# First attention of a float32 block: bf16 thirds on 96 array rows replaced by two rounded f32 halves on 52 rows, with scores and maxima on different halves of the array

## What is computed

```python
qkv = q @ in_proj_weight.T + in_proj_bias          # 4096 x 768
qh, kh, vh = heads of 16 columns, 16 heads
qh = qh / math.sqrt(d)                              # d = 16
scores = jnp.einsum('bhid,bhjd->bhij', qh, kh)      # 4096 x 4096 a head
rel = jnp.clip(pos[None, :] - pos[:, None], -K, K) + K          # K = 64
bias = take_along_axis(einsum('bhid,rd->bhir', qh, rel_pe), rel)
attn = jax.nn.softmax(scores + bias, axis=-1)
out = jnp.einsum('bhij,bhjd->bhid', attn, vh)
```

## Time and profile before

| | us |
|---|---|
| median of 3 runs | 5778.08 (5756.49 to 5778.12) |
| profiled execution, its own time | 5783.44 |
| its span (first to last instruction) | 5781.8 |
| TensorE matmul busy | 5294.7 |
| VectorE busy | 4105.4 |
| ScalarE busy | 3109.6 |
| GpSimd busy | 953.5 |

### The profile page before, as it was taken

How to read it: one execution, slowest core, us unless ns; L and a number is a source line. 1 busy time by engine, 2 the same in 40 slices (tenths; PEclk the granted TensorE clock), 3 DMA queues, 4 the chain that set the end, 5 groups by cost and what they waited for, 6 DMA issues and landing times. The chain is left out here.

```text
span 5781.8 us, 113252 instructions
## 1 busy us (share of the span) xinstructions
PE 5294.7 (92%) x33984; PEld 2681.2 (46%) x33984; DVE 4105.4 (71%) x8598; ACT 3109.6 (54%) x4537; POOL 953.5 (16%) x704
## 2 busy tenths in 40 slices
PE   7499999999999999999999999985999898999895
PEld 3233333333333333333333333332888654888653
DVE  4388888888888888888888888832777433777434
ACT  3256666666666666666666666630555312565310
POOL 0111111111111111111111111101333101333100
PEclk8589999999999999999999999975999899999997
DMA  6511112111111111112111111112000000000000
GB/s 166 141 40 53 48 54 56 48 53 54 50 53 53 48 54 55 48 53 54 50 53 53 47 52 47 52 43 91 1 0 0 16 0 16 1 0 0 30 0 29
DMA packets 203462, 254.49 MB, mean 44 GB/s; under 512 B 71086, under 2 KB 132852, under 8 KB 201588
## 3 DMA queue, kind: packets, MB, share of 16 engines
q1 hardware_dynamic: 199524, 232.98, 14.3%
q0 software_dynamic: 3856, 20.45, 1.3%
HBM read 210.73 MB, written 42.47 MB: 44 GB/s over the span
## 5 line engine op out<-in xcount | busy, mean ns | idle before, releaser
L745 DVE TENSOR_REDUCE group_max<-shared_ps 128x1 f32<-128x512 f32 x4096 | 2684.7, 688 | 586.7 <-PE shared_ps L469 484.2
L622 ACT ACTIVATE probs<-scores 128x1024 f32<-128x1024 f32 x2048 | 2012.3, 1021 | 1052.9 <-PE scores L495 673.7
L469 PE MATMUL shared_ps<-keys,max_queries 96*128 96x512 bf16 x4096 | 1436.1, 385 | 3.2 <-issue 1.7
L495 PE MATMUL scores<-queries,keys 98*128 98x512 bf16 (+3 forms) x4096 | 1218.5, 372 | 86.6 <-ACT probs L622 85.6
L510 PE MATMUL out_ps<-probs,values 128*17 128x512 f32 x8192 | 1089.2, 604 | 0.4 <-ACT probs L622 0.4
L469 PEld LDWEIGHTS shared_ps<-keys,max_queries 96*128 96x128 bf16 x4096 | 396.1, 97 | 1123.5 <-DVE group_max L745 507.9
L215 POOL TENSOR_TENSOR near_window<-near_bias,one_f 128x1536 bf16<-128x1536 f32 x128 | 351.5, 2746 | 2953.7 <-DVE max_parts L739 2305.8
L495 PEld LDWEIGHTS scores<-queries,keys 98*128 98x128 bf16 x4096 | 360.3, 98 | 465.7 <-ACT probs L622 236.9
L1303 PE MATMUL quad<-h_T,w 128*128 128x512 f32 (+1 forms) x768 | 344.3, 599 | 1.9 <-ACT h_T L1417 1.9
L521 PE MATMUL shared_ps<-block_q,block_table 96*128 96x32 bf16 x4096 | 271.5, 233 | 65.2 <-POOL block_q L406 65.2
L521 PEld LDWEIGHTS shared_ps<-block_q,block_table 96*128 96x128 bf16 x4096 | 231.3, 114 | 171.8 <-issue 122.4
(11 more groups left out here) (186 smaller groups left out, 5639.0 us busy)
## 6 DMA issues: line engine op xcount, KB each, us to landing
keys<-k_parts SPq DMA_DIRECT2D x384, 96.0 KB, 2.1
values<-v_wide SPq DMA_DIRECT2D x128, 272.0 KB, 2.7
keys<-k_parts SPq DMA_DIRECT2D x384, 64.0 KB, 2.0
keys<-k_parts SPq DMA_DIRECT2D x128, 132.0 KB, 2.4
q_stack<-part SPq DMA_DIRECT2D x96, 128.0 KB
k_parts<-part SPq DMA_DIRECT2D x96, 128.0 KB
queries<-q_stack SPq DMA_DIRECT2D x128, 96.0 KB, 2.2
max_queries<-q_stack SPq DMA_DIRECT2D x128, 96.0 KB, 2.3
```

The lines of the kernel that those rows point to most:

```text
L469: mm = pe.matmul(bank, max_queries[par][:, t * P:(t + 1) * P], keys[par][0:ROWS, (t + TPC * g) * P:(t + TPC * (g + 1)) * P], start=True, s ...
L495: mm = pe.matmul(out[:, 0:cut], keys[par][:, c * P:(c + 1) * P], queries[par][:, 0:cut], start=True, stop=True)
L622: act.activation(probs[s % 4][:], scores[s % 2][:], ACT.Exp).then_inc(exp_done, 1)
L745: dve.tensor_reduce(group_max[par][:, k:k + 1], bank, AX.X, ALU.max).then_inc(max_read, 1)
```

## The change

q and k are each cut into two values that the f32r format (f32 rounded for a single pass through the array) holds exactly, `high` and `low`. A product is high x high + low x high + high x low, which takes 3 x 16 rows; two rows carry the edge term of the bias (`edge_rows`, from a new small matmul in the projection), two the maximum: 52 rows. The same operands are kept twice, on partitions 0 to 51 and on 64 to 115. Scores use the lower copy, maxima the upper (`max_pair`). The two kinds alternate in the program.

The keys of a head (all 4096) stay on chip for its eight steps; loads are by head. `max_ps` has two slots of two banks, and VectorE reduces both banks with one instruction (`pair_max`, 128x1024), 16 a step in place of 32 of 128x512. `score_ps` is a ring of three single banks that carries scores, the prepared bias and the maximum rows; the exponential is 32 instructions of 128x512 a step in place of 16 of 128x1024. The near columns of the scores are spread over the order of the tiles (`ORDER`). GpSimd copies the maximum row to the second side (`copy_max`). The projection is unrolled and its staging buffers are double; v is stored once. The loop body of `attend` has 16 steps in place of 2. The later stages are the same code.

```diff
@@ -37,13 +37,12 @@
 TPC = CH // P
-Q_PARTS = (0, 0, 0, 1, 1, 2)
 K_RUNS = (3, 2, 1)
 MROWS = 2
+KROWS = 2 * MROWS + 3 * D
 VW = D + 1
 SLAB = 2 * P
...
+    NEAR = (0, 1, 2, 3, 4, TILES - 1)
+    ORDER = [5, 0, 1, 6, 2, 3, 7, 4] + list(range(8, TILES))
+    NEAR_SPAN = {0: (0, 192, 1, 64), 1: (64, 320, 2, 0), 2: (192, 448, 3, 0), 3: (320, 512, 4, 0),
+                 4: (448, 512, 5, 0), TILES - 1: (0, 64, 0, 192)}
+    BIAS_TURN = {0: 0, 1: 1}
+    ROWS_TURN = 4
+    STEP = []
+    for turn in range(QUADS):
+        if turn == ROWS_TURN:
+            STEP.append(("rows", 0))
+        STEP += [("score", (4 * (turn + 2) + i) % TILES) for i in range(4)]
+        if turn in BIAS_TURN:
+            STEP.append(("bias", BIAS_TURN[turn]))
+    STEP.append(None)
+    RING = 3
+    S_START = 2 * NEXT_GEN + 1 + 8
...
-        scores = [ps(f"scores{i}", [P, 2, CH]) for i in range(2)]
+        score_ps = [ps(f"score_ps{i}", [P, CH]) for i in range(RING)]
+        max_ps = [ps(f"max_ps{i}", [P, 2, CH]) for i in range(2)]
...
-        shared_ps = [ps(f"shared_ps{i}", [P, CH]) for i in range(3)]
...
+            def load_keys(h, par):
+                part = k_parts[bass.ds(h, 1)].rearrange("a r n -> (a r) n")
+                for base in (P // 2, 0):
+                    sp.dma_start(keys[par][base + 4:base + 4 + D, :].bitcast(F32), part[0:D]).then_inc(keys_in[par], 16)
+                    sp.dma_start(keys[par][base + 4 + D:base + KROWS, :].bitcast(F32), part).then_inc(keys_in[par], 16)
...
+            def copy_max(m, i):
+                par = i % 2
+                pool.wait_ge(score_read, rows_placed(m, i))
+                pool.tensor_tensor(queries[par][0:MROWS, 1:2, :], queries[par][0:MROWS, 0:1, :].bitcast(F32),
+                                   one_f[0:MROWS].to_broadcast([MROWS, 1, CH]), ALU.mult).then_inc(max_copied, 1)
...
+                c, par, key_par = i % CHUNKS, i % 2, i // CHUNKS
...
+                slot = item % 2
+                for b in range(2):
+                    bank = max_ps[slot][:, b, :]
+                    first = TPC * c + t + 8 * j + 4 * b
+                    near = {(0, 0): [(0, t + 1, P), (1, t + 2, 0)], (3, 1): [(3, t, 2 * P)]}.get((j, b), [])
+                    cuts = [0, 4] if not first < TILES < first + 4 else [0, TILES - first, 4]
+                    for a, z in zip(cuts, cuts[1:]):
+                        side = (first + a) // TILES
+                        tile = (first + a) % TILES
+                        inside = [entry for entry in near if a <= entry[0] < z]
+                        mm = pe.matmul(bank[:, a * P:z * P],
+                                       queries[par][P // 2:P // 2 + KROWS, side, t * P:(t + 1) * P],
+                                       keys[key_par][P // 2:P // 2 + KROWS, tile * P:(tile + z - a) * P],
+                                       start=True, stop=not inside)
+                        for k, (pos, slab, u) in enumerate(inside):
+                            mm = pe.matmul(bank[:, pos * P:(pos + 1) * P], near_window[c % 2][:, slab, u:u + P],
+                                           ident_b[:], start=False, stop=k == len(inside) - 1)
+                    yield b
+                mm.then_inc(max_written, 1)
...
+            def score(m, i, pos, bank):
+                c, par, key_par = i % CHUNKS, i % 2, i // CHUNKS
+                if pos == 0:
+                    pe.wait_ge(score_q_in[par], at_step(m, i // 2 * 2, 24, 48))
+                    pe.wait_ge(score_read, rows_placed(m, i))
...
+                for side, a, z in ((0, 0, cut), (1, cut, CH)):
+                    if a < z:
+                        mm = pe.matmul(bank[:, a:z], keys[key_par][0:KROWS, tile % TILES * P:(tile % TILES + 1) * P],
+                                       queries[par][0:KROWS, side, a:z], start=True, stop=True)
+                mm.then_inc(score_written, 1)
...
+            def sum_quadrants(m, i, item):
+                pe.wait_ge(out_copied, at_step(m, i, 1, 2))
+                pe.wait_ge(max_read, max_before(m, i, PAIRS_M - 1))
                 for t in range(TPC):
-                    mm = pe.matmul(shared("sum", 0)[:, t * VW:(t + 1) * VW], out_copy[:, t * P:(t + 1) * P],
+                    mm = pe.matmul(max_ps[item % 2][:, 0, t * VW:(t + 1) * VW], out_copy[:, t * P:(t + 1) * P],
                                    sum_sel[:], start=True, stop=True)
...
+            def step(m, i, last):
+                n = m * BODY + i
+                at = 0
+                def free(at):
+                    pe.wait_ge(score_read, items_before(m, i, at - 2))
+                    return score_ps[at % RING][:]
                 for turn in range(QUADS):
+                    pv_quad(m, i, turn)
+                    if turn == ROWS_TURN:
+                        if not last or n + 1 < TOTAL:
+                            max_to_rows(*later(m, i, 1), free(at))
+                        at += 1
+                    for half in range(2):
+                        slot = 2 * turn + half
+                        ahead = 1 if slot + LEAD < PAIRS_M else 2
+                        parts = iter((0, 1))
+                        if not last or n + ahead < TOTAL:
+                            pe.wait_ge(max_read, max_before(m, i, slot - 1))
+                            parts = max_pair(*later(m, i, ahead), (slot + LEAD) % PAIRS_M, M_START + i * M_ITEMS + slot)
+                        for k in range(2):
+                            next(parts)
+                            pos = (4 * (turn + 2) + 2 * half + k)
+                            if pos < TILES:
+                                score(m, i, pos, free(at))
+                            elif not last or n + 1 < TOTAL:
+                                score(*later(m, i, 1), pos - TILES, free(at))
+                            at += 1
+                        for _ in parts:
+                            pass
+                    if turn in BIAS_TURN:
+                        if not last or n < LAST_BIAS:
+                            make_bias(m, i + NEXT_GEN, BIAS_TURN[turn], free(at))
+                        at += 1
+                sum_quadrants(m, i, M_START + i * M_ITEMS + PAIRS_M)
...
+            def exp_tile(m, i, pos, bank):
+                if ORDER[pos] in NEAR:
+                    act.wait_ge(near_added, at_step(m, i, len(NEAR), NEAR.index(ORDER[pos]) + 1))
+                act.wait_ge(pv_done, at_step(m, i, QUADS, pos // 4 + 1))
+                act.activation(probs[:, pos % 8, :], bank, ACT.Exp).then_inc(score_read, 1)
...
+                    if at == 1 + STEP.index(("score", 5)):
+                        act.wait_ge(pv_done, at_step(m, i, QUADS, QUADS + 2))
+                        act.wait_ge(max_written, max_before(m, i, 0))
                         act.activation(out_copy[:], out_ps[:], ACT.Copy).then_inc(out_copied, 1)
...
-            def bank_max(n, par, k, bank):
-                dve.wait_ge(max_ready, n * MAX_GROUPS + k + 1)
-                dve.tensor_reduce(group_max[par][:, k:k + 1], bank, AX.X, ALU.max
...
+            def pair_max(m, i, p, item, written):
+                t, j = p % TPC, p // TPC
+                dve.wait_ge(max_written, written)
+                dve.tensor_reduce(group_max[i % 2][:, t, j:j + 1], max_ps[item % 2][:], AX.XY, ALU.max
                                   ).then_inc(max_read, 1)
...
+            def near_adds(m, i, last, turn, half):
+                n = m * BODY + i
+                for k in range(2):
+                    pos = 4 * (turn + 2) + 2 * half + k
+                    ahead, pos = pos // TILES, pos % TILES
+                    if ORDER[pos] in NEAR and (not last or n + ahead < TOTAL):
+                        at = STEP.index(("score", pos))
+                        near_add(*later(m, i, ahead), ORDER[pos], items_before(m, i, at) + 1, at)
...
+                for slot in range(PAIRS_M):
+                    near_adds(m, i, last, slot // 2, slot % 2)
+                    ahead = 1 if slot + LEAD < PAIRS_M else 2
+                    if not last or n + ahead < TOTAL:
+                        pair_max(*later(m, i, ahead), (slot + LEAD) % PAIRS_M, M_START + i * M_ITEMS + slot,
+                                 max_before(m, i, slot + 1))
+                    if not last or n + 1 < TOTAL:
+                        if slot == PAIRS_M - LEAD - 1:
+                            find_max(*later(m, i, 1), max_before(m, i, PAIRS_M - LEAD))
+                        if slot == PAIRS_M - LEAD:
+                            cut_max(*later(m, i, 1))
+                finish(m, i, M_START + i * M_ITEMS + PAIRS_M)
```

928 lines of the change are left out of this document (465 added, 463 removed).

## The result

| | before | after |
|---|---|---|
| median, us | 5769.46 (5756.49 to 5778.12, 4 runs) | 7217.08 (7175.04 to 7229.46, 4 runs) |
| profiled span, us | 5781.8 | 7227.7 |
| granted clock over the span | 0.945 | 0.706 |

The changed kernel takes 1.2499 times as long, with a 95% interval of 1.2439 to 1.2559. 5594 was predicted, so the forecast was wrong in sign and far outside its range.

A forecast was written before the change was run, and what follows sets the result against it. TensorE was taken to bind, VectorE next. A step of 24.7 us plus 1.7 for the clock gave 26.4 against 27.65; 5783.4 - 149 - 45 + 10 = 5599, less 5 is 5594 us, range 5340 to 5760.

The forecast's parts named there:

- Part 1: TensorE in a step: maximum and score overlap fully, 0.23 us together in f32r; 18.9 us a step.
- the near places: Eight places a step where full-row near matmuls break the alternation: 0 to 1.0 us for switches, taken as 0.5.
- Part 2: VectorE in a step: paired reductions of 1.13 us, 21.1 us in all, more than TensorE needs.
- Part 3: ScalarE in a step: 512-column exponentials at 0.49 us, or 0.59; hidden under the step except at the end.
- Part 4: The step walked turn by turn, with slot waits and the boundary: 24.7 us at full clock, a plain turn 2.35.
- the third rival: Each score waits for its own bank of three, or two clock falls a step: about 5740 us, chance 0.14.
- part 6: Outside the attention loop: projection 45 us shorter, the stretch before the loop 10 us longer.
- Part 5: Granted clock in the loop: one half-clock fall of 3.4 us a step, costing 1.7 us, step 26.4.
- Half clock throughout: Rival: TensorE at half clock needs some 35 us a step, over 6600 us; chance 0.03.
- The halves don't overlap: Rival, at the alternation in `step`: TensorE needs 0.23 us for each of 64 matmuls, 5880 us; chance 0.13.
- The clock stays up: Rival: no clock fall in the loop, 24.7 us a step, 5392 us; chance 0.17.
- Waits in line: Scores wait in order for three banks, a second half-clock stretch in turn 1; step 27.3 to 27.9, chance 0.14.

The follow-up runs named there:

- a_near: Changed kernel with the near matmuls of a pair of banks moved behind both maxima and both scores, except where a bank is split: 6242.82 us.
- c_flat4: Changed kernel with 64 rows, near matmuls behind the pairs, all 128 steps written out, four dense matmuls ahead of the sum of quadrants: 5728.65 us, ratio 0.9941.
- b_few: Kernel before, bf16, with maxima on rows 64 to 95 and scores on rows 64 to 97, the same half of the array: 8801.13 us.
- a_onehalf: Changed kernel with the maxima on the same half as the scores, with queries of their own, so nothing overlaps: 9024.24 us, ratio 1.5655.
- a_rows64: Changed kernel with every maximum and score matmul widened from 52 to 64 rows, key copies against zero query rows: 6263.83 us.
- a_twice: Changed kernel with every maximum and score matmul issued twice into the same bank: 6747.45 us.
- the gap matmuls: Dense 128-row matmuls whose result nobody reads, ahead of the sum of quadrants; two of them in the changed kernel alone: 6691.17 us.
- c_gap2: Changed kernel with 64 rows, near matmuls behind the pairs and two dense matmuls ahead of the sum of quadrants, still looped: 5862.20 us, ratio 1.0166.
- c_flat: Changed kernel with 64 rows, near matmuls behind the pairs, two dense matmuls ahead of the sum, all 128 steps written out: 5882.88 us, ratio 1.0182.

## Why the prediction was wrong

- **Part 1, matmuls.** The overlap was right (pairs 0.23 apart, starting together), and so was the price of f32r. The "nothing if free, 8 x 0.12 = 1.0 us at most" for the near places was wrong: it priced a switch of mode, where the loss is the pair that is torn apart, 0.63 us for a place where a pair alone takes 0.33. a_near, which only moves them (27.1 against 28.3 us at full clock), and c_flat4 (turns of 2.76 and 2.82 us against 3.06 and 3.24) show it. After each quad the first pair takes 0.33 and not 0.23.
- **Part 2, VectorE.** 1.22 us a reduction of 128x1024, and 1.14 from one to the next where two ran in a row, as walked. It was not what bound a plain turn: over the program it was idle for 2092 us ahead of them.
- **Part 3, ScalarE.** 0.598 us is how long one exponential takes, but four in a row (from 4648.23) take 2.07 us, 0.49 from one to the next, so the first value was right. "Hidden, except at the end" was wrong: at full clock the fourth score of a plain turn waits for the exponential of the first.
- **Part 4, the step.** At full clock 28.3 and not 24.7. Turns 0 and 1 took 7.7 (6.3 walked), turns 2 to 5 12.8 (10.5), turns 6 and 7 with the boundary 7.8 (7.9). The error lies where the near places are and in the plain turns, 2.6 in place of 2.35. The plain turn is 0.98 for the quad, 0.33, 0.24 and 0.23 to the next three pairs, 0.39 from the fourth maximum to its score and 0.43 for that score alone. The walk let TensorE wait for VectorE's slots and never for `score_ps`; the wait is the one that the third rival names, each score for its own bank of three. By the 28.3 us of this one step, the new kernel would have been slower than the 27.40 of before even with the clock up: an estimated 127 x 0.9 us, less part 6, some 85 us. The mis-sized terms are the near places, the 0.1 us after each quad, and the wait of the fourth score.
- **Part 5, the clock: the step that failed.** "I expect one fall a step, as long as this one (3.4 us ...)": the fall came, at the place named, but it lasted 24 to 38 us in most steps and not 3.4, so that 10.7 us a step and not 1.7 lie above the full-clock step. The reasoning read the fall in the earlier trace rows by gaps and by the sum's 17 columns, and never asked how many rows the matmuls name. The change cuts that, by its own description, from 96 and 98 rows to 52 for the same columns. b_few and a_onehalf show that alone to give half clock at a busy TensorE; a_rows64, a_twice and the gap matmuls give the clock back by the reverse. "Half clock throughout", at 0.03, was the rival that came nearest (0.61 over the loop, 39.0 us a step where it had 35), and "the rise at dense work speaks against it" was the wrong reading: the dense work was of 98 rows.
- **Part 6, outside the loop.** The loop began 27.5 us earlier, against 35 forecast, and what lies behind it kept its length (1954.2 and 1958.1 us). Nearly right. What no part mentioned is the jump back of a body of 16 steps, five standstills of 6.5 to 7.9 us in the changed kernel.
- **The rivals.** "The halves don't overlap" is out. "The clock stays up" had its test in c_flat4: with the clock at 0.99 the step is 27.0, four of the dense matmuls included, and not 24.7. "Waits in line" happened as to the wait, in the plain turn shown, but its 27.3 to 27.9 us are far below the 39.0 measured.

Open: why the steps written out in a row, only 0.5 us shorter, lose the clock so much more often than the looped ones with the same two matmuls; why seven dense matmuls leave more falls than four; and what a ring of four banks would do to the plain turn, which no run tried.

## What to carry to other kernels

Before you let a matmul use fewer rows, or overlap two halves to save TensorE time, ask how full the array stays on average, and read the granted clock beside the busy time: a TensorE that is 97% busy at 0.61 is not the same engine. Saved array work can be paid back in clock; if it is, pad the contraction with zero rows and keep the overlapping pairs unbroken. Here that brought back 1194 of the 1448 us lost, and only with the dense matmuls and the steps in a row did the change gain at all, 0.6%. Then look for the stretch ahead of each fall and put idle-time matmuls there, as many as cost less than the falls do. With the steps in a row four did better here than two or seven.

## What the runs showed of the hardware

- TensorE can be busy for 998 of 1000 us and be granted 0.52 (b_few); the rows that the instructions name, and with them the values, are the only difference from 0.99.
- Rows whose products are all zero count as well: 0.61 became 0.90 with twelve of them a half.
- Doubled matmuls shortened a program, 7217 to 6747 us.
- One or two matmuls on all rows between two on different halves cost the overlap of both neighbours: that place took 0.63 us at full clock, where a pair by itself took 0.23 to 0.33.
- A loop body of 16 steps stood still at its jump for 6.5 to 7.9 us in one kernel (the changed one) and 11.0 to 12.9 in a close relative (c_gap2); steps in a row showed no such stop (c_flat).
